# Attention over eight batches: a loop written out, and the inverse deviation of the output groups moved to POOL as a power

## What is computed

```python
x = L0_attn_x                                  # (8, 1024, 256)
xn = _layernorm(x, axis=-1)
x = x + _L0_attn_ref(xn, ...) + _L0_ffn_ref(xn, ...)

# in _L0_attn_ref: 16 heads of 16, two score maps each
attn = softmax(A1) - lamb * softmax(A2)        # A1, A2: Q1 K1', Q2 K2' * scaling
out = einsum('bhqk,bhkd->bhqd', attn, V).transpose(...).reshape(B, S, DIM) @ Wo
mu, var = mean(out, -1), var(out, -1)
out = (out - mu) * rsqrt(var + LN_EPS) * gamma + beta
```

## Time and profile before

| what | value |
|---|---|
| median of 3 runs | 4272.05 us (4268.96 to 4272.66) |
| span of the profiled execution, first to last instruction | 4262.0 us |
| PE busy | 3874.9 us, 91% of the span |
| DVE busy | 3105.8 us, 73% |
| ACT busy | 2850.4 us, 67% |
| POOL busy | 1328.1 us, 31% |
| TensorE clock granted, mean of the core | 0.953 |
| exponentials L1320, all | 2048, 2161.2 us, mean 1110 ns |
| row maxima L1516, all | 4096, 2597.0 us, mean 683 ns |

### The profile page before, as it was taken

One profiled execution on the slowest core, in us unless ns is written; L12 is line 12 of the kernel. 1 busy time (PEld: TensorE's weight loads), 2 busy tenths in 40 slices (PEclk: granted clock), 3 DMA queues, 4 the chain that ended last, 5 costly groups with the idle time before them and its releaser, 6 DMA issues. The chain is left out here.

```text
span 4262.0 us, 76116 instructions
## 1 busy us (share of the span) xinstructions
PE 3874.9 (91%) x23970; PEld 1577.6 (37%) x23970; DVE 3105.8 (73%) x5547; ACT 2850.4 (67%) x3429; POOL 1328.1 (31%) x1618
## 2 busy tenths in 40 slices
PE   3379999999999999999999999999999949979999
PEld 2123223323323233233223323322332215668888
DVE  3568897898788878987997888788889613434444
ACT  0017887888788878877887888788888946722221
POOL 4211421232134214221421233133214137763420
PEclk8669999999999999999999999999999979989999
DMA  9720111111111111111211111111111029842320
GB/s 317 251 65 24 51 58 42 41 56 40 48 36 56 46 36 47 62 54 32 65 36 51 36 53 39 47 41 59 55 36 58 24 106 359 276 125 90 99 80 20
DMA packets 224807, 332.04 MB, mean 78 GB/s; under 512 B 29297, under 2 KB 165236, under 8 KB 219780
## 3 DMA queue, kind: packets, MB, share of 16 engines
q1 hardware_dynamic: 205956, 276.47, 19.8%
q0 software_dynamic: 18432, 50.36, 3.6%
HBM read 169.34 MB, written 156.34 MB: 76 GB/s over the span
## 5 line engine op out<-in xcount | busy, mean ns | idle before, releaser
L1516 DVE TENSOR_REDUCE arena<-psum 128x1 f32<-128x512 f32 x4096 | 2597.0, 683 | 481.4 <-PE psum L1089 445.4
L1320 ACT ACTIVATE arena<-psum,arena 128x1024 f32<-128x1024 f32 x2048 | 2161.2, 1110 | 193.9 <-PE psum L1127 170.3
L1089 PE MATMUL psum<-arena 48*128 48x512 f16 x4096 | 1385.7, 395 | 80.4 <-DVE arena L1516 22.4
L1143 PE MATMUL psum<-arena 128*32 128x512 f32 x8200 | 1109.5, 613 | 1.4 <-ACT arena L1244 0.7
L1089 PEld LDWEIGHTS psum<-arena 48*128 48x128 f16 x4096 | 323.0, 93 | 1648.5 <-DVE arena L1516 1116.8
L1127 PE MATMUL psum<-arena 50*128 50x512 f16 x4096 | 877.8, 384 | 50.6 <-issue 28.1
L1382 POOL TENSOR_TENSOR arena<-arena 128x16 f32<-128x16 f32 x129 | 28.6, 222 | 1779.4 <-DVE arena L1526 1779.4
L1075 PE MATMUL psum<-arena 128*128 128x256 f32 x1024 | 291.2, 410 | 11.0 <-DVE arena L1516 11.0
L749 ACT ACTIVATE mix_arena<-psum,mix_arena 128x1024 f32<-128x1024 f32 x64 | 71.3, 1114 | 321.8 <-DVE mix_arena L769 321.8
L1252 ACT ACTIVATE arena<-psum,arena 128x256 f32<-128x256 f32 x256 | 121.2, 474 | 230.6 <-PE psum L1075 230.3
L1127 PEld LDWEIGHTS psum<-arena 50*128 50x128 f16 x4096 | 210.1, 94 | 167.7 <-ACT arena L1320 89.9
(11 more groups left out here) (165 smaller groups left out, 3040.5 us busy)
## 6 DMA issues: line engine op xcount, KB each, us to landing
arena<-scratch_split SPq DMA_DIRECT2D x768, 64.0 KB, 2.1
scratch_split<-arena SPq DMA_DIRECT2D x64, 512.0 KB, 3.2
scratch_sorted_x<-route_arena SPq DMA_DIRECT2D x60, 512.0 KB, 8.1
leaf_arena<-scratch_sorted_x SPq DMA_DIRECT2D x60, 512.0 KB, 6.0
scratch_sorted_y<-leaf_arena SPq DMA_DIRECT2D x60, 512.0 KB, 4.1
leaf_arena<-in_leafw SPq DMA_DIRECT2D x3, 5128.0 KB, 19.3
arena<-in_x SPq DMA_DIRECT2D x18, 512.0 KB, 4.3
scratch_sum<-arena SPq DMA_DIRECT2D x18, 512.0 KB, 3.0
```

Source lines behind the costliest of these rows:

```text
L1089: nc.tensor.matmul(aux_bank[bank], ring[at, slot, 0, m, qt * P:(qt + 1) * P], ring[at, slot, 1, m, c * CH:(c + 1) * CH], start=True, stop=True
L1143: last = nc.tensor.matmul(value_bank[32 * j:32 * j + 32, :], vaug[:, kt, 2 * (s % PER_BATCH) + j % 2, :], prob[:, step % 2, j, :], start=k ...
L1320: nc.scalar.activation(prob[:, step % 2, 2 * h:2 * h + 2, :], score[:, 2 * h:2 * h + 2, :], ACT.Exp, scale=exp_scale[:, s % 2, s // 2:s // ...
L1516: nc.vector.tensor_reduce(halfmax[:, odd, 2 * m + h, qt, c:c + 1], aux_bank[bank], AX.X, ALU.max).then_inc(bank_used[bank], 1)
```

## The change

The loop of each engine becomes a Python `for` over all eight batches, so each batch has instructions of its own with constants in them. `guess_std` and `inverse_std` are gone. `finish` on POOL now waits for the variance, raises it to the power -0.5 (128x4), does the Newton step in four instructions of 128x4, and goes on as before; each waits for the one ahead of it. The `memset` of `tmp` in `stats` is gone too.

```diff
@@ the same on sp, pe, act, pool and dve
-            with pe.Fori(0, LAST) as i:
-                body(i, False)
-            body(LAST, True)
+            for i in range(BATCH):
+                body(i, i == LAST)
@@ act: body
-                        for h in range(2):
-                            if (s, step) == (1, 2 if h == 0 else 15):
-                                groups[h].guess_std(nc, act, i)
@@ dve: body, and the same after the last batch
-                            if (s, step) == (1 + h, 4):
-                                groups[h].inverse_std(nc, dve, link, i)
@@ OutputGroup
-    def guess_std(self, nc, act, n):
-        act.wait_ge(self.var_ready, n + 1)
-        nc.scalar.activation(self.guess, self.var, ACT.Sqrt).then_inc(self.guess_ready, 1)
...
-    def inverse_std(self, nc, dve, link, n):
...
     def finish(self, nc, pool, n):
-        pool.wait_ge(self.rstd_ready, n + 1)
+        done = n * self.POOL_LINKS
+        pool.wait_ge(self.var_ready, n + 1)
         wide = [P, self.G, DIM]
+        nc.gpsimd.tensor_tensor(self.rstd, self.var, self.power, ALU.pow).then_inc(self.pchain, 1)
+        pool.wait_ge(self.pchain, done + 1)
+        nc.gpsimd.tensor_tensor(self.tmp, self.rstd, self.rstd, ALU.mult).then_inc(self.pchain, 1)
+        pool.wait_ge(self.pchain, done + 2)
+        nc.gpsimd.tensor_tensor(self.tmp, self.tmp, self.var, ALU.mult).then_inc(self.pchain, 1)
+        pool.wait_ge(self.pchain, done + 3)
+        nc.gpsimd.tensor_scalar(self.tmp, self.tmp, -0.5, 1.5, ALU.mult, ALU.add).then_inc(self.pchain, 1)
+        pool.wait_ge(self.pchain, done + 4)
+        nc.gpsimd.tensor_tensor(self.rstd, self.rstd, self.tmp, ALU.mult).then_inc(self.pchain, 1)
+        pool.wait_ge(self.pchain, done + 5)
         nc.gpsimd.tensor_tensor(self.y, self.y, self.mv[:, :, 0:1].to_broadcast(wide), ALU.subtract
                                 ).then_inc(self.pchain, 1)
```

More of the change, by code:

```diff
@@ L1025, in body @@
                 group = [2 * batch, 2 * batch + 1]
-                if not tail:
-                    group = [sp.snap(group[0]), sp.snap(group[1])]
                 for s in range(PER_BATCH):
@@ L1248, in read_qk @@
                 a, c = number // (QK_UNITS // 2), number % (QK_UNITS // 2)
-                if not (isinstance(t, int) and t == 0):
+                if t > 0:
                     act.wait_ge(split_ready, t * 4 + (number // 2 - 3))
@@ L1259, in read_shift @@
             def read_shift(n, bank):
-                if not (isinstance(n, int) and n == 0):
+                if n > 0:
                     act.wait_ge(shift_in, n * 64)
@@ L1332, in body @@
                             k += 1
-                        for h in range(2):
-                            if (s, step) == (1, 2 if h == 0 else 15):
-                                groups[h].guess_std(nc, act, i)
-            with act.Fori(0, LAST) as i:
-                body(i, False)
-            body(LAST, True)
+            for i in range(BATCH):
+                body(i, i == LAST)
             copy_values(LAST, PER_BATCH - 1, 1)
@@ L1347, in _ @@
                     read_group(BATCH, kind, number, bank)
-            for h in range(2):
-                groups[h].guess_std(nc, act, BATCH)
         @block.gpsimd
@@ L1356, in split_parts @@
                 cols = slice(c * CH, (c + 1) * CH)
-                if number == 0 and not isinstance(t, int):
+                if number == 0 and t > 0:
                     pool.wait_ge(split_stored, t * 32)
-                if isinstance(t, int) and t == 1 and number == 0:
-                    pool.wait_ge(split_stored, 32)
                 nc.gpsimd.tensor_tensor(split[:, a, 0, cols], rest[:, a, cols], zeros[:, 0:CH], ALU.add
@@ L1429, in body @@
                             scatter(n // NFFF, n % NFFF)
-            with pool.Fori(0, LAST) as i:
-                body(i, False)
-            body(LAST, True)
+            for i in range(BATCH):
+                body(i, i == LAST)
             join_maps(BATCH * 2 * PER_BATCH, PER_BATCH - 1, 1)
@@ L1486, in _ @@
                 nc.vector.memset(groups[h].var, 0.0).then_inc(groups[h].y_ready, 1)
-                nc.vector.memset(groups[h].guess, 0.0).then_inc(groups[h].stored, 1)
+                nc.vector.memset(groups[h].power, -0.5).then_inc(groups[h].stored, 1)
             link(nc.vector.memset(halves, 0.0))
@@ L1565, in body @@
                                 groups[h].stats(nc, link)
-                            if (s, step) == (1 + h, 4):
-                                groups[h].inverse_std(nc, dve, link, i)
-            with dve.Fori(0, LAST) as i:
-                body(i, False)
-            body(LAST, True)
+            for i in range(BATCH):
+                body(i, i == LAST)
             link = Chain(dve, dchain, BATCH * per_iter + links_before)
@@ L1577, in _ @@
                 groups[h].stats(nc, link)
-                groups[h].inverse_std(nc, dve, link, BATCH)
 class GroupConsts:
@@ L1599 @@
     G = 4
-    LINKS = 2 + 4
+    LINKS = 2
+    POOL_LINKS = 9
     def __init__(self, nc, ctx, ar, consts, prefix):
@@ L1609, in __init__ @@
         self.mv = ar.take(G, 2)
-        self.var, self.guess, self.rstd, self.tmp = ar.take(G), ar.take(G), ar.take(G), ar.take(G)
+        self.var, self.power, self.rstd, self.tmp = ar.take(G), ar.take(G), ar.take(G), ar.take(G)
         def sem(name):
@@ L1657, in stats @@
         link(ins)
-        nc.vector.memset(self.tmp, 0.0)
         for q in range(self.G):
@@ L1681, in finish @@
         nc.gpsimd.tensor_tensor(self.y, self.y, self.rstd.unsqueeze(2).to_broadcast(wide), ALU.mult
                                 ).then_inc(self.pchain, 1)
[L1683 removed]
+        pool.wait_ge(self.pchain, done + 7)
         nc.gpsimd.tensor_tensor(self.y, self.y, self.consts.gamma.unsqueeze(1).to_broadcast(wide), ALU.mult
                                 ).then_inc(self.pchain, 1)
[L1686 removed]
+        pool.wait_ge(self.pchain, done + 8)
```

7 lines of the change are left out of this document (3 added, 4 removed).

## The result

The changed kernel takes 4169.19 us (median of 4 runs, 4164.72 to 4171.66) against 4270.51 us before (4 runs, 4266.13 to 4272.66): a ratio of 0.9763, 95% interval 0.975 to 0.9777. The forecast was 4171 us and faster, so both the side and the size hold. The terms behind it did not all hold, and one of them failed.

A forecast was written before the change was run, and what follows sets the result against it. Plain attention steps were held by DVE's row maxima, others by PE, ACT and a PSUM bank; odd steps cost extra. Gains of 53 + 11 + 28.5 + 7.2 + 1 = 100.7 us gave 4171 us, range 4146 to 4206.

The forecast's parts named there:

- Returns: Loop's return, (7, 15) to (0, 2) of the next batch: six returns go at 8.8 us each, 53 us gained.
- That rival: At the batch borders, straight code stalls like the branch, so the 53 us stay: 4224 us, chance 5%.
- Registers: Register instructions in all sets of the loop's batches: 0.2 us a set over 7 batches, 11 us gained.
- First square root: Steps (1, 2) to (1, 7): 4.2 us go in five batches and 2.5 in three, 28.5 us gained.
- Second square root: Border of sets 1 and 2: loads covered by DVE, inverse_std's 0.9 us a batch goes, 7.2 +- 8.8 us.
- The meeting of L1662 with POOL: DVE's L1662 took 1.28 us while POOL ran finish; new POOL instructions shift this by up to 1.1 us either way.
- the rival on the other side: POOL's power is long, so PE waits for split_max once a batch; gain used up at 14.3 us, chance 5%.
- The rival by which every load lies on the path: At the square roots, every table load counts in full: 45 us, 25 us more gain, 4146 us, chance 4%.
- Epilogue: After batch 7, where nothing hides POOL: 5.4 us go, new instructions add 4.4, 1 us gained.
- the high end: Slow end of the forecast's range, 4206 us: clock still falling, no register gain, worse meeting, power of 5 us in epilogue.
- The 10.05 us from span to median: Difference between the earlier kernel's span of 4262.0 us and its median of 4272.05 us, carried over unchanged.

The follow-up runs named there:

- the fastest kernel: Changed kernel with the LN_EPS addition moved from DVE to POOL and statistics of three of a group's four pieces each taken two steps after reading: 4127.51 us.

## Why the prediction was right, and which step of it was not

- **Returns.** Right in size and mechanism: 53.3 us for 53. Straight code does not stall like the branch; all seven borders take 10.04 us. That rival is out.
- **Registers.** 12.2 us less the 1.9 at (2, 6), and 1.0 more for (1, 6), where sets 0 and 3 show the same gain: 11.3 us for 11. The estimate of 0.2 a set, from set 3 inside and outside the loop, carried over: former loop batches gained 1.7 us each in these steps and batch 7 0.2. The loop on ACT alone shows whose they are.
- **First square root.** 31.0 us for 28.5 (30.0 without the register's part). The wait of the statistics stayed, as forecast, at 1.44 us for 1.46. The clock had fallen in six batches of before, not five, in one of them (batch 5) earlier, in step (1, 2), at a stretch of 21.03 us.
- **Second square root, the step that failed.** "Their cost is covered by DVE, and the 0.9 us of `inverse_std` goes" was right for `inverse_std` by 5.7 of 7.2 us. Against it the steps behind the addition lost 3.9 us, and with the 1.9 us of (2, 6) counted elsewhere -0.1 us was left of the term. The meeting of L1662 with POOL was named, and priced at 1.1 us either way as unknown; at an equal clock it took some 1.1 us of the 3.9. That it would be held longer could have been had: the rule of it stood in the epilogue of before, and with it the order of POOL's instructions gives where the pass lies. The other 2.8 us are PE's clock at this border, which the sum has at nothing without a reason: it prices the clock at the first square root alone. The result is inside the 7.2 +- 8.8 given for the term.
- **POOL.** The power is 1.04 us, so the rival on the other side, which needs 14.3 us, is out. Its slack was read rightly: six more powers use it up.
- **Table loads.** The rival by which every load lies on the path would have given 45 us for the square roots; the power alone gained 31.9.
- **Epilogue.** 0.9 us for 1: from variance to POOL's last pass 27.66 us before and 26.72 after.
- **Slips of the working.** A power of 7 us gives 4199 us by the forecast's own sum, not 4190; the high end adds up to 4207, not 4206; and 7.4 - 1.1 - 1.2 leaves 5.1 us for the power, not 5.0. Nothing hangs on them.

That the total came within 2 us of the median has luck in it: the terms of the batches were off by +0.3, +2.5, -7.3 and +1.2 us, which is -3.3, and the difference between spans (92.1) and medians (101.3) is larger than that. The 10.05 us from span to median, carried over unchanged, were no constant: each run of the changed kernel lies 1.8 us above its span (4171.66 and 4169.9), so most of them was the distance of the profiled execution of before from its median.

## What to carry to other kernels

A loop's cost at its return is not the sum of what its engines lose there: compare the last turn inside the loop with the same work outside it, and expect nothing from unrolling one engine while another still returns. Where a change lengthens POOL's list, look which small DVE additions and multiplications from SBUF to SBUF then fall into a wide pass of POOL, because each of them lasts until that pass ends. And where four small operations in a row stall a paced loop, spread them over steps with slack: that was worth 21 to 24 us here (4151.3 to 4127.5, and 116.4 to 137.7 of gain against the kernel before of each round).

## What the runs showed of the hardware that I had not expected

- A 128x4 addition on DVE takes 0.17 us alone and up to 1.62 us beside a 128x1024 pass of POOL, and ends within 0.03 us of that pass. A reciprocal of 128x4 takes 0.18 us inside such a pass.
- A loop's return costs 8.2 us on PE alone (49.5 / 6), 4.9 on DVE and 3.5 on ACT, and 8.9 (53.3 / 6) with all five engines in it; PE's lower clock is in these figures.
- The instructions that set a semaphore's number from a register cost ACT 9.6 us over seven batches, DVE 1.6 and PE 0.7.
- A stall of PE can cost more than its own length: with 26.3 us of waits for POOL in batches 1 to 7, and none of them longer than 3.5 us, steps (2, 6) to (3, 6) of the kernel with six more powers lost 40 us in these seven batches, and the granted clock fell to half behind the waits. In the fastest kernel it stayed at 1.0 for 2890 us.
